# Self attention of a transformer layer: the transpose of the maxima moved to the head of its step, the next group's maxima begun there

## The reference

```python
qkv = x @ qkv_w.T
q, k, v = jnp.split(qkv, 3, axis=-1)
scores = jnp.einsum('bhqd,bhkd->bhqk', q, kh) / jnp.sqrt(jnp.float32(D))
...
scores = jnp.where(allowed_pos[None, None], scores, NEG)
scores = jnp.where(causal[None, None], -jnp.inf, scores)
p = jax.nn.softmax(scores, axis=-1)
out = jnp.einsum('bhqk,bhkd->bhqd', p, vh)
```

## Time and profile before

| what | us |
|---|---|
| median of 3 runs (lowest to highest) | 3167.23 (3163.73 to 3175.45) |
| the profiled execution: its own time | 3164.31 |
| its span in the trace | 3162.6 |
| TensorE busy in the span | 2977.9 |
| VectorE, GpSimd, ScalarE busy | 1756.2, 1892.8, 1242.1 |
| self attention: first and last transpose of maxima start at | 508.2, 1079.0 |

### The profile page before, as it was taken

The page is one execution under the profiler, slowest core; times in us unless marked ns, Lnnn a source line. Parts: engine busy times, 40 slices in busy tenths (PEclk is TensorE's granted clock), DMA queues, the critical chain, the costliest instruction groups (busy, mean ns, idle before and its releaser), DMA issues.

```text
span 3162.6 us, 39517 instructions
## 1 busy us (share of the span) xinstructions
PE 2977.9 (94%) x15266; PEld 1966.4 (62%) x15266; DVE 1756.2 (56%) x2868; ACT 1242.1 (39%) x2335; POOL 1892.8 (60%) x984
## 2 busy tenths in 40 slices
PE   9999999999999959899999999999879999999999
PEld 7888886444444437664444444444348888888887
DVE  5456556777777535667777777777642222222221
ACT  3123223555555523226666666666532111111111
POOL 4234334888887864438888888888758343333422
PEclk9999999999999979999999999999989999999999
DMA  7555764555555037634242342422122101011000
GB/s 261 170 178 173 225 212 105 110 117 115 116 116 115 25 117 225 201 122 99 54 102 60 71 92 54 98 65 71 42 94 63 40 27 41 14 40 40 27 14 14
DMA packets 199538, 310.17 MB, mean 98 GB/s; under 512 B 15011, under 2 KB 93363, under 8 KB 199347
## 3 DMA queue, kind: packets, MB, share of 16 engines
q1 hardware_dynamic: 199350, 307.64, 35.5%
HBM read 189.04 MB, written 117.44 MB: 97 GB/s over the span
## 4 chain that ended last, share of the span: by engine, by line
PE 54%; DVE 5%; DMA 2%; POOL 1%; issue 1%; ACT 1%; SPq 0%; DVEq 0%; ACTq 0%
PE m_ring L89 14%; PE m_o_ps L89 11%; PE e_st L1224 8%; PE e_pv L1236 7%; PE e_nat L1207 7%; PE c_ring L89 5%; PE e_st L1250 3%; DVE e_neg_max L1117 2%; DMA e_qs<-e_max_lo 1%; DMA c_x<-in_x 1%; DVE m_xn L1575 0%; DMA c_w_raw<-in_ca_in_w 0%; DVE m_xt_lo L1582 0%; POOL m_hid_lo L1550 0%; ACT c_xt L660 0%
## 5 line engine op out<-in xcount | busy, mean ns | idle before, releaser
L1061 POOL TENSOR_TENSOR e_probs<-e_probs 128x2048 f32<-128x2048 f32 x159 | 727.3, 4581 | 137.8 <-ACT e_probs L1036 133.1
L1036 ACT ACTIVATE e_probs<-e_st 128x512 f32<-128x512 f32 x1024 | 557.8, 598 | 366.4 <-PE e_st L1224 348.6
L1117 DVE TENSOR_REDUCE e_neg_max<-e_nat 128x1 f32<-128x1024 f32 x512 | 602.7, 1216 | 140.1 <-PE e_nat L1207 135.2
L1036 ACT ACTIVATE b_probs<-b_st 128x512 f32<-128x512 f32 (+3 forms) x768 | 340.3, 490 | 277.3 <-PE b_st L1224 267.2
L1114 DVE CUSTOM_DVE_ANT_0 b_nat<-b_nat,mask_qk 128x128 f32<-128x128 f32 (+7 forms) x512 | 374.1, 783 | 80.9 <-PE b_nat L1207 79.7
L1224 PE MATMUL e_st<-e_qs,e_ks 98*128 98x512 f32 x1024 | 396.0, 431 | 10.1 <-DMA e_qs<-e_max_lo 7.5
L1550 POOL TENSOR_TENSOR m_hid_lo<-m_hid,m_hid_hi 128x512 fp32r<-128x512 f32 x128 | 168.2, 1314 | 383.6 <-DVE m_hid_hi L1588 383.6
L1061 POOL TENSOR_TENSOR b_probs<-b_probs 128x1536 f32<-128x1536 f32 (+3 forms) x126 | 371.0, 2945 | 37.8 <-PE b_pv L1236 35.1
L1588 DVE CAST m_hid_hi<-m_hid 128x512 fp32r<-128x512 f32 x128 | 60.9, 475 | 574.4 <-ACT m_hid L1469 574.4
L1207 PE MATMUL e_nat<-e_ks,e_qs 96*128 96x512 f32 x1024 | 327.0, 400 | 21.8 <-DVE e_neg_max L1117 21.8
L1224 PEld LDWEIGHTS e_st<-e_qs,e_ks 98*128 98x128 f32 x1024 | 176.0, 189 | 263.0 <-ACT e_probs L1036 190.9
(11 more groups left out here) (183 smaller groups left out, 5154.6 us busy)
## 6 DMA issues: line engine op xcount, KB each, us to landing
b_qs<-sq_hi SPq DMA_DIRECT2D x32, 512.0 KB, 6.8
b_ks<-sk_hi SPq DMA_DIRECT2D x32, 512.0 KB, 11.2
e_qs<-cq_hi SPq DMA_DIRECT2D x32, 512.0 KB, 6.7
e_ks<-ck_hi SPq DMA_DIRECT2D x32, 512.0 KB, 13.5
ck_hi<-p_part_hi SPq DMA_DIRECT2D x32, 256.0 KB, 3.4
ck_lo<-p_part_lo SPq DMA_DIRECT2D x32, 256.0 KB, 3.7
cv<-p_tok_out SPq DMA_DIRECT2D x32, 256.0 KB, 3.2
p_x<-in_x SPq DMA_DIRECT2D x8, 1024.0 KB, 7.5
```

The lines of the kernel that those rows point to most:

```text
L1036: act.activation(probs[:, home(n, k), j, first:TOK], st_ps[:, bank_at("scores", blk), first:TOK], ACT.Exp).then_inc(exped, 1)
L1061: pool.tensor_tensor(into, into, probs[:, home(n, k), :, first:TOK], ALU.add).then_inc(added, 1)
L1117: dve.tensor_reduce(neg_max[:, u:u + 1], found, AX.XY, ALU.max, negate=True).then_inc(maxed, 1)
```

## The change

One line of `attention`. In the self attention TURN_HEAD (VectorE's split) and PE_TURN_HEAD (TensorE's transpose) become 0 instead of 2; the cross attention keeps 2 and 3.

```diff
@@ -827,7 +827,7 @@
     NS, NBLOCKS = len(steps), len(steps) * HG
     UNITS = HG * KT
-    TURN, TURN_HEAD, PE_TURN_HEAD, TURN_BANK = NS - 3, 2, 2 if causal else 3, 2
+    TURN, TURN_HEAD, PE_TURN_HEAD, TURN_BANK = NS - 3, 0 if causal else 2, 0 if causal else 3, 2
```

## The result

The changed kernel takes 3187.51 us (median of 5 runs, 3183.83 to 3192.42) against 3167.23 (5 runs, 3162.67 to 3175.45): 20.3 us more, a ratio of 1.0063 with a 95% interval of 1.0049 to 1.0078. The forecast was 3190, the range 3176 to 3204.

The account below looks back on a forecast made before the run. TensorE, busy 94% of the span, was taken as the bound, only its idle time movable. 15 groups x (1.6 - 0.1) = +22.5, rounded to +23, gave 3190 us on the median (+0.7%), range 3176 to 3204.

Parts of the forecast that it names:

- Stretch B: Small sum's start to next group's first weigh, 16.95 us: GpSimd's gapless chain limits the fall to 0.18, booked -0.1 a group.
- Rival 1: Self attention: the transpose's wait is simply gone, 15.1 us come off, giving 3152 us; chance 0.05.
- Unit 2's new wait: Behind the early transpose, TensorE's unit 2 waits for VectorE's split: 0.5 us new.
- Stretch A: Large sum's end to small sum's start, 13.43 us: bank waits and moved units add 1.75, taken as 1.6 a group.
- unit 21's wait: Between the large and small sums, unit 21 waits 0.64 us for unit 19's reduction to free its bank.
- The others: Between the large and small sums, bank waits of units 22, 26 and 30: 0.68, 1.0 and 0.55 us.
- the sum of before's waits: Waiting between the sums before the change: three bracketed waits plus issue time behind them, 1.70 us, subtracted from the new waits.
- the distance: Start of one group's transpose to the next in the self attention: 39.5 to 39.7 us expected instead of 38.05.
- C: The rest of a group's interval, 7.7 us, holding units 14 to 16 instead of 12 to 14: -0.06 us, booked as nothing.
- The tail and the first group: End of the projections, where group 1's units 5 and 6 issue earlier: 0 to +2 us, taken as 0.
- Rival 3: Self attention: new waits also make the clock fall once a group, +25 us, giving 3215 us; chance 0.07.
- The late issues: Matmuls behind a wait on TensorE take 0.10 us more each; 0.40 for four between the large and small sums.

Follow-up runs that it names:

- experiment 1: The kernel before the change, with VectorE reducing only the first half of the keys of each group's last three units (29 to 31): 3164.8 us, ratio 0.9987.
- experiment 2: The kernel before the change, with those halved reductions and GpSimd's addition of step 7 made for one head of four: 3154.1 us, ratio 0.9950.
- experiment 3: The kernel before the change, with only GpSimd's addition of step 7 made for one head of four: 3165.2 us, ratio 0.9986 to that kernel.
- experiment 4: The changed kernel, with GpSimd's addition of step 7 made for one head of four: 3169.4 us, ratio 1.0002 to the kernel before.
- experiment 5: The changed kernel, with units 26 and 27 moved behind the weigh of step 6: 3178.2 us, ratio 1.0027 to the kernel before.
- experiment 8: The changed kernel, with units spread over all heads of the steps and transpose and split a step later: 3128.3 us, ratio 0.9874 to the kernel before.
- experiment 6: The changed kernel's places for units 12 to 31, but transpose and split as before the change: 3195.1 us, ratio 1.0087 to the kernel before.
- experiment 7: Transpose and split early as in the change, units 17 to 30 placed as before it, unit 15 earlier: 3172.9 us, ratio 1.0017 to the kernel before.

## Why the prediction was right, and where a size was off

**Stretch B, the wait removed.** Right in mechanism and size. Of the transpose's wait 0.2 was expected to be left, and 0.16 is. B fell by 0.10, bounded at 0.18, booked at 0.1. Experiments 1 to 4 make the square: the transpose's wait shortened gives 0.10 with GpSimd's chain whole and 0.52 with it shortened; the chain shortened gives nothing before and 0.83 in the change. Rival 1 (the wait is simply gone, -15 us) fell with that. One sentence goes too far: that TensorE is not what sets this stretch. Before the change it did, with the transpose's wait in it (experiment 3: B 16.96 without GpSimd's chain); GpSimd sets it only once that wait has shrunk by 0.10. Unit 2's new wait was put at 0.5 and is 0.40 in brackets, unit 10's at 1.0 and is 0.97.

**Stretch A, the waits that grow.** Right in place, somewhat too large: 1.75 worked out, 1.6 taken, 1.38 measured. Two terms were mis-sized. The first is unit 21's wait, 0.64 in the walk. In issue time it was 0.45 (0.29 + 0.16), for two reasons. VectorE was done 0.08 earlier, since unit 17's reduction, the first behind the inversion, took 0.32 instead of 0.38 us (922.91 to 923.23) and the next 0.51. And TensorE came 0.11 later than walked (923.84 + 0.29 = 924.13, which is 3.03 behind the large sum's end and not 2.92); that part is work in place of waiting and does not shorten A. The others, 0.68, 1.0 and 0.55, came out as 0.65, 1.08 and 0.57, 0.07 more together. The second is the sum of before's waits. I took the three rows in brackets, but the kernel before had a fourth wait, inside a merged row (units 27 and 28, and the score behind them):

```profile
918.16 1.03 PE L1207 MATMUL b_nat<-b_ks,b_qs 97*128 97x512 f32 x3
919.03 0.39 PE L1224 MATMUL b_st<-b_qs,b_ks 99*128 99x512 f32 x1
```

From 918.16 to 919.03 are 0.87 us for 0.24 + 0.29 of work: unit 28 had waited about 0.24, with 0.10 for the late issue. With these corrections the walk gives 1.75 - 0.08 + 0.07 - 0.34 = 1.40, for 1.38 found. That A's waits are waits for a bank at too short a distance, and not VectorE's load, is shown by 5, where A holds the same units and is 14.0, and by 8, where the load of the whole interval is the same and the units' waits are 2.0 us in all instead of 46.6. That they come from where the units stand and not from the transpose is shown by 6.

Of what the next profile should show, two figures missed with this term: the distance, 39.30 for 39.5 to 39.7, and the units' waits, 46.6 us for over 50.

**Elsewhere.** C was booked at nothing and is -0.04. The tail and the first group were put at 0 to +2 us. The profile's first interval is 41.5 against 37.65, with the clock at half there:

```profile
520.00:527.00 7.00, 7.00 (x28) 0.51 1.01 214
527.00:534.00 7.00, 6.59 (x46) 1.00 1.05 202
```

Experiment 5, with the same order in the tail of the projections and the first steps, has 37.65 there and no such fall, while experiment 6 has 42.2 and one; the order alone does not decide it, and what does was not tried. The profiled execution's 24.5 us add up as 20.9 between the first and the last transpose (591.6 for 570.8), 0.2 for what lies ahead of the first and the rest of the last group together (-2.6 and +2.8, since the transpose stands earlier in its group), and 3.4 behind the self attention, where both kernels have the same order. On the medians it is 20.3. The sum (22.5, rounded up to 23) less the 0.26 us a group by which the net was over, 1.5 for 1.24, is 18.6; the median lies 1.7 above that, within the runs' scatter.

**Rival 3, the clock,** did not decide: behind its first interval the change ran at 1.00 (700 to 1050, for one). Its mechanism is real, though, as 7 shows.

**The late issues and the second chain.** The Trainium skill (TensorE: Matmul & The Clock Gate, "Step-by-step: what each phase is for") says that weight loads are pulled ahead of matmuls in flight; by that the late issues would be free. The rows go on showing 0.10 us behind a wait (0.67 for 97x448 x2 at 925.92, 0.57 without a wait elsewhere in the same group), so here the measurement decides. The Trainium skill (Perfetto Trace Analysis, "Optimization Strategy") advises making what a gap waits for start sooner. Done here it took 1.0 us of gap away and gave 0.10 us, and experiments 1 to 3 show why: a second chain ended right behind the first. The loss beside it is another thing, the units that moved along.

## What to carry to other kernels

Before a wait is removed, ask which chain ends next behind it at the point where the stretch is closed; here GpSimd's, on an engine busy 60% of the time, came 0.10 us behind and took the rest of the gain. When a planner's origin is shifted, everything it lays out moves: cost the new neighbours, above all the distance between an instruction that fills a bank and the one that needs it back, and spread those out before anything else (1.26% in experiment 8, with the same instructions in another order). Count waits from start to start too, since merged rows hide some.

## What was not expected of the hardware

The granted clock fell to half behind a single wait of only 1.1 us in experiment 7 (889 to 896: 0.55), and three times more in that loop; five of its 15 intervals are longer for it. In the change it fell in the first interval, behind a wait of 0.98 us at 518.41 (520 to 527: 0.51), but the later groups, with waits of 0.97 and 0.92 us and more waiting in all, kept 1.00. What told these apart was not tried. The other point is small: a reduction on VectorE that starts behind another kind of operation was 0.03 to 0.06 us shorter than one behind a reduction (in the kernel before, 1024 keys took 1.12 us behind the inversion, 908.62 to 909.74, and 1.18 behind a reduction, 915.92 to 917.10).
